# Mixture-of-experts stages: the down product in two-part rounded fp32, weighted by GpSimd

## The chip, the cores and the metric

One core of one Trainium2 chip runs the whole program. The metric is the time of one execution on the device in microseconds; lower is better. The engines are named as the profile names them: PE (TensorE), ACT (ScalarE), DVE (VectorE), POOL (GpSimd) and SP (SyncE, which only issues transfers).

## The reference

A chain of four parts works on 2048 tokens of 128 numbers: a gated layer with running sums (`_L0_attn_a`), two transformer layers (`_L0_ffn`), a non-causal attention (`_L0_attn_b`), and the same two transformer layers again. A transformer layer is causal attention and then a mixture of 8 experts, of which two count:

```python
def _ffn(h, w1, b1, w2, b2):
    return gelu(h @ w1 + b1, approximate=False) @ w2 + b2      # 128 -> 512 -> 128

def _combine_weights(logits):                                  # top 2 of 8, softmax over the two
    vals, idx = top_k(logits, 2)
    w = softmax(vals)
    return sum(w[..., None] * onehot(idx, 8), axis=-2)

def _token_moe(h, ...):                                        # layer 0: per token
    cw = _combine_weights(h @ gw + gb)
    for e in range(8):
        out = out + _ffn(h, w1[e], b1[e], w2[e], b2[e]) * cw[..., e:e + 1]

def _seq_moe(h, ...):                                          # layer 1: one choice for the sequence
    cw = _combine_weights(h.mean(axis=1) @ gw + gb)
    ...
```

All is fp32. Layer 0 computes all eight experts for all tokens and weights them; layer 1 computes only the two that were chosen.

## The kernel before

The program is a row of stages, each with its own semaphores and a barrier at its end. `feed_forward` runs, for each of its two layers, `project_qkv`, `attention_heads`, `finish_attention` and `experts`; it is called twice, with the tag f and with the tag g, and a stage for the separate attention (tag b) lies between. So `experts` runs four times: token-routed (f, then g) and sequence-routed (f, then g). Tiles of the two layers of one tag have the same names in the profile.

`experts` works on four chunks of 512 tokens. First DVE normalises all 16 tiles of 128 tokens into `e_hn`; PE transposes them chunk by chunk into `e_ps_turn`; ACT writes h once into `e_h_hi` as rounded fp32 (`F32R`) and once in place, and DVE subtracts the first from the second to get `e_h_lo` (line 1470). The router's logits follow: 48 small matmuls in the token-routed stage, one in the other, then a chain of small DVE operations (`top2`) that picks the two best.

Then comes a hardware loop over the four chunks (`Fori`), whose body is written out for all blocks. A block is one of the four parts of 128 hidden units of one expert; a chunk has 32 blocks in the token-routed stage and 8 in the other. For block k, PE runs `up(k)`: three matmuls (lines 1559 to 1561), weights stationary, 512 tokens moving: `w1_hi` with `h_hi`, `w1_lo` with `h_hi`, `w1_hi` with `h_lo`. ACT makes the gelu out of PSUM into `e_hidden` (line 1656), plain fp32. Three blocks later PE runs `down(k-3)`: four fp32 matmuls (line 1609), one for each 128 tokens, with the hidden tile stationary and w2 moving, so that the result has the tokens on the partitions. The profile shows each fp32 matmul as two records. After the four blocks of an expert DVE multiplies the sum by the token's combine weight and adds it to `z_tok` (line 1516). The bias b2 comes in by a matmul of the transposed combine weights with the 8 rows of b2 (line 1626) and an addition by DVE (line 1533). In the token-routed stage the combine weights are finished chunk by chunk, with ACT's Exp (line 1660) in each pass.

w2 of the token-routed layer is loaded once, in the set-up (line 201 of the source), and kept in SBUF. In the sequence-routed stage SP loads w1, w2 and b1 of each of the two chosen experts, and DVE waits for all six transfers before it splits both w1 in one go (lines 1500 and 1501).

The semaphores of a stage are cleared by GpSimd at the start of the next (`clear_previous`), ahead of its own work there, which in `project_qkv` and `experts` is `rstd` (line 304), on which the normalisation waits.

## Time and profile before

| | us |
|---|---|
| median of 3 runs | 3347.49 (3345.98 to 3355.19) |
| profiled execution, its own time | 3349.13 |
| its span | 3347.4 |

| engine | busy us | share of the span |
|---|---|---|
| PE matmul | 2748.5 | 82% |
| PE weight load | 1299.9 | 39% |
| DVE | 2337.0 | 70% |
| ACT | 2171.7 | 65% |
| POOL | 331.7 | 10% |

The four `experts` stages lie, with their matmuls, at about 616 to 847 and 2569 to 2799 us (token-routed) and 1306 to 1387 and 3259 to 3343 us (sequence-routed); the last one ends the program. The shares over the whole span say little about them, since attention, which fills most of it, has other limits. What counts is the busy time of each engine inside a stretch of one stage, the granted clock there (1.00 is 2.4 GHz, 0.50 is 1.2 GHz), and at the edges of a stage the order in time of single rows. A matmul's own duration holds its latency; the pace of PE is read from one start to the next.

### The profile page before, as it was taken

To read this page: it belongs to the slowest core of one execution; us is meant where nothing else is said; L and a number is where in the kernel's file an instruction comes from. 1 tells how busy PE (TensorE), PEld (TensorE's weight loads), DVE (VectorE), ACT (ScalarE), POOL (GpSimd) and SP (SyncE) were. 2 spreads that over 40 slices of the span, in tenths; PEclk is the share of its full clock that TensorE was granted. 3 is DMA by queue.
4 is the path that set the end of the run, shared out by engine and by line. 5 is a ranking of instruction groups with operands and counts; after the bars stand their busy time and mean duration, and the time that the engine had idled before them with its cause. 6 is when DMAs were issued, how large, how long until landed. Compare 5 with 4: busy or idle time off the path is not lost. (4 is left out here: it accounts for less than half of the span.)

```text
span 3347.4 us, 75365 instructions
## 1 busy us (share of the span) xinstructions
PE 2748.5 (82%) x29824; PEld 1299.9 (39%) x29824; DVE 2337.0 (70%) x3203; ACT 2171.7 (65%) x4160; POOL 331.7 (10%) x868
## 2 busy tenths in 40 slices
PE   4459999699499994859999998389996996799967
PEld 3322332599333332612222222233333995233326
DVE  5659997322499993469999996499993223799953
ACT  1137889354278983339999998168884453588853
POOL 3023110000031100000000000031100000221000
PEclk8669999799699997969999999699997998799988
DMA  2060000000500001140000000600001003200010
GB/s 56 7 142 27 13 11 8 30 0 0 126 21 15 10 10 45 40 88 8 10 8 10 8 8 25 138 18 16 12 10 32 1 0 75 65 18 11 10 34 25
DMA packets 96737, 99.80 MB, mean 30 GB/s; under 512 B 13158, under 2 KB 84644, under 8 KB 96420
## 3 DMA queue, kind: packets, MB, share of 16 engines
q1 hardware_dynamic: 79140, 77.62, 8.8%
q10 hardware_dynamic: 16640, 15.73, 1.9%
q8 instruction: 214, 3.51, 0.5%
q0 software_dynamic: 640, 2.10, 0.2%
q14 instruction: 103, 0.84, 0.1%
HBM read 51.44 MB, written 43.65 MB: 28 GB/s over the span
## 5 line engine op out<-in xcount | busy, mean ns | idle before, releaser
L1189 ACT ACTIVATE h_probsf<-h_ps_scoresf 128x512 f32<-128x512 f32 (+3 forms) x1216 | 603.5, 552 | 155.3 <-PE h_ps_scoresf L1141 142.9
L1189 ACT ACTIVATE h_probsg<-h_ps_scoresg 128x512 f32<-128x512 f32 (+3 forms) x1216 | 603.6, 552 | 150.8 <-PE h_ps_scoresg L1141 138.3
L1189 ACT ACTIVATE h_probsb<-h_ps_scoresb 128x512 f32<-128x512 f32 x1024 | 556.3, 596 | 73.8 <-PE h_ps_scoresb L1141 63.8
L1163 PE MATMUL h_ps_valuesf<-h_probsf,v_all 128*9 128x256 f32 (+2 forms) x4608 | 348.8, 375 | 29.5 <-POOL h_probsf L1252 21.9
L1163 PE MATMUL h_ps_valuesg<-h_probsg,v_all 128*9 128x256 f32 (+2 forms) x4608 | 347.5, 374 | 26.3 <-POOL h_probsg L1252 18.6
L1163 PE MATMUL h_ps_valuesb<-h_probsb,v_all 128*9 128x256 f32 x4096 | 318.4, 383 | 9.4 <-ACT h_drainedb L1196 4.8
L1212 DVE TENSOR_REDUCE h_maxima_0b<-h_ps_scanb 128x2 f32<-128x1024 f32 x256 | 292.5, 1217 | 10.9 <-PE h_ps_scanb L1103 9.6
L1212 DVE TENSOR_REDUCE h_maxima_2b<-h_ps_scanb 128x2 f32<-128x1024 f32 x256 | 292.8, 1217 | 6.7 <-PE h_ps_scanb L1103 6.7
L1103 PE MATMUL h_ps_scanf<-k_stack,q_stack 48*128 48x512 bf16 (+3 forms) x1280 | 218.1, 363 | 69.9 <-DVE h_ps_valuesf L1201 51.5
L1212 DVE TENSOR_REDUCE h_maxima_0f<-h_ps_scanf 128x2 f32<-128x1024 f32 x224 | 259.2, 1219 | 22.6 <-PE h_ps_scanf L1103 22.3
L1103 PE MATMUL h_ps_scang<-k_stack,q_stack 48*128 48x512 bf16 (+3 forms) x1280 | 217.0, 361 | 70.3 <-DVE h_ps_valuesg L1201 50.4
L1212 DVE TENSOR_REDUCE h_maxima_0g<-h_ps_scang 128x2 f32<-128x1024 f32 x224 | 259.0, 1219 | 20.5 <-PE h_ps_scang L1103 20.2
L1141 PE MATMUL h_ps_scoresf<-q_stack,k_stack 49*128 49x256 bf16 (+2 forms) x2048 | 228.0, 286 | 13.2 <-ACT h_probsf L1189 7.2
L1141 PE MATMUL h_ps_scoresg<-q_stack,k_stack 49*128 49x256 bf16 (+2 forms) x2048 | 227.9, 286 | 12.6 <-ACT h_probsg L1189 6.8
L1103 PE MATMUL h_ps_scanb<-k_stack,q_stack 48*128 48x512 bf16 x1024 | 200.7, 390 | 37.9 <-DVE h_ps_valuesb L1201 21.7
L1141 PE MATMUL h_ps_scoresb<-q_stack,k_stack 49*128 49x256 bf16 x2048 | 201.6, 275 | 15.0 <-ACT h_probsb L1189 14.7
L1212 DVE TENSOR_REDUCE h_maxima_2f<-h_ps_scanf 128x2 f32<-128x1024 f32 x160 | 185.6, 1219 | 12.7 <-PE h_ps_scanf L1103 11.6
L1212 DVE TENSOR_REDUCE h_maxima_2g<-h_ps_scang 128x2 f32<-128x1024 f32 x160 | 185.6, 1219 | 12.7 <-PE h_ps_scang L1103 11.6
L1252 POOL TENSOR_SCALAR_AFFINE_SELECT h_probsg<-h_probsg 128x128 f32<-128x128 f32 (+1 forms) x384 | 122.9, 332 | 621.5 <-ACT h_probsg L1189 614.5
L1252 POOL TENSOR_SCALAR_AFFINE_SELECT h_probsf<-h_probsf 128x128 f32<-128x128 f32 (+1 forms) x384 | 122.0, 332 | 598.3 <-ACT h_probsf L1189 591.4
L1141 PEld LDWEIGHTS h_ps_scoresf<-q_stack,k_stack 49*128 49x128 bf16 x2048 | 66.3, 94 | 261.5 <-ACT h_probsf L1189 238.9
L1141 PEld LDWEIGHTS h_ps_scoresg<-q_stack,k_stack 49*128 49x128 bf16 x2048 | 66.3, 94 | 259.5 <-ACT h_probsg L1189 239.7
(423 smaller groups left out, 3865.9 us busy)
## 6 DMA issues: line engine op xcount, KB each, us to landing
q_stack<-q_parts ACTq DMA_DIRECT2D x20, 256.0 KB, 8.3
k_stack<-k_parts ACTq DMA_DIRECT2D x20, 256.0 KB, 9.8
q_stack<-q_parts SPq DMA_DIRECT2D x20, 256.0 KB, 8.8
k_stack<-k_parts SPq DMA_DIRECT2D x20, 256.0 KB, 10.7
attended<-h_drainedf SPq DMA_DIRECT2D x16, 256.0 KB, 2.3
attended<-h_drainedf SPq DMA_DIRECT2D x32, 128.0 KB, 1.9
attended<-h_drainedb SPq DMA_DIRECT2D x32, 128.0 KB, 1.9
attended<-h_drainedg SPq DMA_DIRECT2D x16, 256.0 KB, 2.2
```

The source lines that it names most:

```text
L1103: last = nc.tensor.matmul(ps_scan[:, i % RING_A, b, at:at + width], m.q_stack[rows, c, 2 * quad + hp, t * P:(t + 1) * P], m.k_stack[rows, ...
L1141: last[b] = nc.tensor.matmul(ps_scores[:, (2 * n_pair + b) % RING_S, width * i + off:width * (i + 1)], m.k_stack[rows, kb // TPC, pair, at ...
L1163: last = nc.tensor.matmul(ps_values[32 * j:32 * j + VD, low:high], m.v_all[:, kb, QUAD * quad + j, :], probs[:, (u + j % banks) % RING_P, ...
L1189: nc.scalar.activation(by_head(probs[:, of % RING_P, :], of), by_head(ps_scores[:, of % RING_S, :], of), ACT.Exp, scale=SOFTMAX_SCALE).the ...
L1212: nc.vector.tensor_reduce(found[:, :, low], now, AXIS_X, ALU.max).then_inc(freed, 1)
L1252: nc.gpsimd.affine_select(out=at, in_=at, compare_op=ALU.is_ge, fill=0.0, base=0, pattern=[[0, at.shape[1]], [1, P]], channel_multiplier=- ...
```

## The change

- The down product is computed as the up product is: `w2_hi` and `w2_lo` stationary, the hidden tile split in `hidden_hi` and `hidden_lo` moving, three matmuls of 512 columns. The result has the 128 output dimensions on the partitions.
- The split of the hidden tile: for even blocks ACT makes the gelu in place in PSUM and DVE rounds it (`high`); for odd blocks ACT makes it twice, into `hidden_hi` and in place. DVE subtracts (`low`) for all blocks.
- w2 is loaded in each stage into two buffers and split by GpSimd.
- ACT moves an expert's result out of PSUM with b2 as bias (`evacuate`). In the token-routed stage GpSimd multiplies it by the combine weights and adds it up over the experts. The weights of a chunk are transposed, written to DRAM, and read back spread over all partitions, one row of 512 for each expert. In the sequence-routed stage the weight is the scale of the evacuation, and GpSimd adds the two experts.
- PE transposes the sum of a chunk back (`turn_back`), and DVE adds it to `z`. The b2 matmuls, the additions per expert and the statistics after the last stage are gone.
- All combine weights are finished at once, in blocks 3 to 6 of the first chunk.
- The order: four ups run ahead of the downs (three before); in the token-routed stage they stand ahead of the logits. The hardware loop is gone; all blocks are written out. Normalising is done by chunks in two buffers.
- In the sequence-routed stage the two w1 are asked for first, then the biases, then w2; each w1 is split when it is in.
- Many small tiles are put into the space of `q_stack`; `w_qkv`, `w_swiglu` and `w_out` are kept only as long as they are used. In the profile such tiles go by the name `q_stack`.

```diff
@@ set_up
-            rest.append((m.b2[:, :, :], ins["L0_ffn_e_b2"].rearrange("l e d -> e l d")))
-            sp.dma_start(m.w2[:, :, :, :], ins["L0_ffn_e_w2"][0].rearrange("e (i p) d -> p (e i) d", p=P))
+                     (rows[E_B2:N_VEC, :], ins["L0_ffn_e_b2"][0])]
@@ experts
+RING_H, RING_SPLIT, RING_CW, RING_W2 = 4, 4, 4, 2
+LAG = 4
+CW_AT, TURN_BACK_AT = 8, 8
@@ gpsimd
+            for e in range(n_exp):
+                pool.wait_ge(w2_in[e], 16)
+                now = raw_w2[:, e % RING_W2, :]
+                nc.gpsimd.tensor_copy(w2_hi[:, e, :], now).then_inc(w2_high, 1)
+                pool.wait_ge(w2_high, e + 1)
+                nc.gpsimd.tensor_tensor(w2_lo[:, e, :], now, w2_hi[:, e, :].bitcast(F32), ALU.subtract)
+            for y in range(CHUNKS * n_exp):
+                c, e = y // n_exp, y % n_exp
+                pool.wait_ge(evacuated, y + 1)
...
+                if by_token:
+                    pool.wait_ge(cw_in[y % RING_CW], 16 * (y // RING_CW + 1))
+                    nc.gpsimd.tensor_tensor(part, y_sb[:, y % 2, :], cw_rows[:, y % RING_CW, :], ALU.mult)
+                    if e:
+                        nc.gpsimd.tensor_tensor(acc[:, c % 2, :], acc[:, c % 2, :], part, ALU.add)
+                elif e:
+                    nc.gpsimd.tensor_tensor(acc[:, c % 2, :], y_sb[:, 0, :], y_sb[:, 1, :], ALU.add)
@@ vector
+            def high(k):
+                dve.wait_ge(gelu_ready, k + 1)
+                if k >= RING_SPLIT:
+                    dve.wait_ge(down_ready, k + 1 - RING_SPLIT)
+                nc.vector.tensor_copy(hidden_hi[:, k % RING_SPLIT, :], ps_h[:, k % RING_H, :])
+            def low(k):
+                nc.vector.tensor_tensor(hidden_lo[:, k % RING_SPLIT, :], ps_h[:, k % RING_H, :],
+                                        hidden_hi[:, k % RING_SPLIT, :].bitcast(F32), ALU.subtract)
...
+            for k in range(total):
+                if k % 2 == 0:
+                    high(k)
+                low(k)
+                if by_token and k == 3:
+                    choose()
+                if by_token and k == 6:
+                    combine()
@@ tensor
-                    for r in range(TPC):
-                        q = slice(r * P, (r + 1) * P)
-                        last_ = nc.tensor.matmul(ps_y[:, e % 2, r, :], hidden[:, k % ring_h, q], w2[:, e, b, :],
-                                                 start=b == 0 and r == 0, stop=b == FB - 1, skip_group_check=True)
+                product(ps_y[:, y % 2, :], (w2_hi[:, e, b * D:(b + 1) * D], w2_lo[:, e, b * D:(b + 1) * D]),
+                        (hidden_hi[:, k % RING_SPLIT, :], hidden_lo[:, k % RING_SPLIT, :]), b == 0, b == FB - 1)
...
+            for k in range(RING_H, total):
+                up(k)
+                down(k - LAG)
+                if by_token and k == CW_AT:
+                    turn_cw(0)
+                if by_token and k % blocks == 2 * CW_AT and k // blocks + 1 < CHUNKS:
+                    turn_cw(k // blocks + 1)
+                if k >= blocks and k % blocks == TURN_BACK_AT - 1:
+                    turn_back(k // blocks - 1)
@@ scalar
+            def gelu(k):
+                act.wait_ge(up_ready, k + 1)
+                if k % 2:
+                    if k >= RING_SPLIT:
+                        act.wait_ge(down_ready, k + 1 - RING_SPLIT)
+                    nc.scalar.activation(hidden_hi[:, k % RING_SPLIT, :], ps_h[:, k % RING_H, :], ACT.Gelu, bias=bias)
+                    act.wait_ge(high_by_act, k // 2 + 1)
+                nc.scalar.activation(ps_h[:, k % RING_H, :], ps_h[:, k % RING_H, :], ACT.Gelu, bias=bias)
+            def evacuate(y):
+                act.wait_ge(down_ready, FB * (y + 1))
+                if y >= 2:
+                    act.wait_ge(weighted, y - 1)
+                nc.scalar.activation(y_sb[:, y % 2, :], ps_y[:, y % 2, :], ACT.Identity, ...)
```

PE, in the first token-routed stage, inside the loop: two blocks of before. `e_ps_h` is the PSUM tile of an up product, `e_ps_y` that of a down product, the letter f at a name's end the tag.

```order
1255 L1609 MATMUL e_ps_yf<-w,e_hiddenf 128x128 x4
1256 L1559 MATMUL e_ps_hf<-e_h_hif,w_hi 128x512
1257 L1560 MATMUL e_ps_hf<-e_h_hif,w_lo 128x512
1258 L1561 MATMUL e_ps_hf<-e_h_lof,w_hi 128x512
1259 L1603 REGISTER_ALU
1260 L1609 MATMUL e_ps_yf<-w,e_hiddenf 128x128 x4
```

The same place now, from the last logit on; four ups have run before the logits.

```order
1240 L1608 MATMUL e_ps_turnf<-gate_hi,e_h_hif 128x8
1241 L1609 MATMUL e_ps_turnf<-gate_hi,e_h_lof 128x8
1242 L1610 MATMUL e_ps_turnf<-gate_lo,e_h_hif 128x8
1243 L1608 MATMUL e_ps_hf<-e_h_hif,w_hi 128x512
1244 L1609 MATMUL e_ps_hf<-e_h_hif,w_lo 128x512
1245 L1610 MATMUL e_ps_hf<-e_h_lof,w_hi 128x512
1246 L1608 MATMUL e_ps_yf<-e_hidden_hif,e_w_hif 128x512
1247 L1609 MATMUL e_ps_yf<-e_hidden_hif,e_w_lof 128x512
1248 L1610 MATMUL e_ps_yf<-e_hidden_lof,e_w_hif 128x512
```

The four matmuls of 128 columns have become three of 512, and the first down follows the first up behind the logits at once.

SP, in the sequence-routed stage of f, before: the loads of the first chosen expert, then a register load for the second.

```order
217 L1672 TENSOR_LOAD ids_int
218 L1672 ISA x2
219 L1673 ISA
220 L1673 DMA e_raw_w1f<-in_L_ffn_e_w 128x512
221 L1675 DMA e_w2f<-in_L_ffn_e_w 128x4x128
222 L1677 ISA
223 L1677 DMA e_b1f<-in_L_ffn_e_b 128x4x1
224 L1672 TENSOR_LOAD ids_int
```

And now, behind both register loads:

```order
232 L1795 DMA q_stack<-in_L_ffn_e_w 128x512
233 L1795 ISA
234 L1795 DMA q_stack<-in_L_ffn_e_w 128x512
235 L1798 ISA
236 L1798 DMA e_b1f<-in_L_ffn_e_b 128x4x1
237 L1800 ISA
238 L1800 DMA e_b2f<-in_L_ffn_e_b 128x1
239 L1798 ISA
240 L1798 DMA e_b1f<-in_L_ffn_e_b 128x4x1
241 L1800 ISA
242 L1800 DMA e_b2f<-in_L_ffn_e_b 128x1
243 L1803 DMA q_stack<-in_L_ffn_e_w 128x4x128 x2
```

Both w1 stand first and both w2 last.

POOL, at the start of the projection that follows a token-routed stage, before and now; the ISA rows are the semaphores that `clear_previous` clears.

```order
109 L1404 UNCONDITIONAL_BRANCH
110 L644 UNCONDITIONAL_BRANCH
111 L95 ISA x29
112 L304 TENSOR_TENSOR rstd<-p_tmpb,neg_half 128x16
113 L587 UNCONDITIONAL_BRANCH
```

```order
159 L1394 UNCONDITIONAL_BRANCH
160 L640 UNCONDITIONAL_BRANCH
161 L96 ISA x51
162 L300 TENSOR_TENSOR rstd<-p_tmpf,neg_half 128x16
163 L583 UNCONDITIONAL_BRANCH
```

Ahead of `rstd` there were 29 such instructions behind each of the first three `experts` stages (the rows of before are those behind a sequence-routed one); now there are 51 behind a token-routed stage and 45 behind the sequence-routed one.

## Rows read from the trace of the kernel before

**Rows 1.** Stretches of the token-routed stage: busy time (count) by engine, clock, DMA.
```profile
625.00:635.00 10.00, 10.00 (x48) 10.00 (x49) 0.00 (x0) 0.30 (x1) 0.00 (x0) 0.50 0.01 2
635.00:639.00 4.00, 4.00 (x10) 3.16 (x11) 3.41 (x12) 1.38 (x2) 0.00 (x0) 0.50 0.00 0
639.00:690.00 51.00, 51.00 (x359) 46.68 (x358) 10.01 (x37) 25.04 (x35) 0.00 (x0) 1.00 0.00 1
```

**Rows 2.** Timeline: start us, duration us, engine, line, operation.
```profile
690.15 0.39 PE L1559 MATMUL e_ps_hf<-e_h_hif,w_hi 128*128 x1
...
690.85 0.40 PE L1559 MATMUL e_ps_hf<-e_h_hif,w_hi 128*128 x1
...
839.11 0.48 PE L1559 MATMUL e_ps_hf<-e_h_hif,w_hi 128*128 x1
...
840.69 0.48 PE L1559 MATMUL e_ps_hf<-e_h_hif,w_hi 128*128 x1
```

**Rows 3.** Groups by line, ACT, 600 to 870 us: busy us, mean ns | idle before.
```profile
L1656 ACT ACTIVATE e_hiddenf<-e_ps_hf,vecs 128x512 f32<-128x512 f32 x128 | 87.6, 688 | 113.3 <-PE e_ps_hf L1561 113.0
...
L1660 ACT ACT_TABLE_LOAD x4 | 5.1, 1283 | 0.1
...
L1638 ACT ACTIVATE e_h_hif<-e_ps_turnf,vecs 128x512 fp32r<-128x512 f32 x4 | 3.1, 773 | 30.3 <-PE e_ps_turnf L1553 30.3
```

**Rows 4.** Groups by line and form, DVE, whole span.
```profile
L1470 DVE TENSOR_TENSOR e_h_lof<-e_ps_turnf,e_h_hif 128x512 fp32r<-128x512 f32 x8 | 5.5, 690 | 6.1 <-ACT e_ps_turnf L1641 6.1
...
L443 DVE TENSOR_SCALAR a_ega<-a_ps_paira 128x512 f32<-128x512 f32 x4 | 2.8, 692 | 0.2
...
L452 DVE TENSOR_SCALAR a_ega<-a_ega 128x512 f32<-128x512 f32 x4 | 1.7, 414 | 0.0
```

**Rows 5.** Groups by line and form, POOL, whole span.
```profile
L1034 POOL TENSOR_TENSOR w_lo<-h_raw_weightsf,w_hi 128x512 fp32r<-128x512 f32 x8 | 10.1, 1269 | 0.7
...
L1032 POOL CAST w_hi<-h_raw_weightsf 128x512 fp32r<-128x512 f32 x8 | 4.9, 611 | 7.0 <-DMA h_raw_weightsf<-in_L_ffn_e_w 7.0
```

**Rows 6.** Timeline, end of the token-routed stage and start of the next projection.
```profile
843.04 3.73 PE L1609 MATMUL e_ps_yf<-w,e_hiddenf 128*128 128x128 f32 x32
...
849.35 0.19 DVE L292 TENSOR_TENSOR p_tmpf<-st 128x16 f32<-128x16 f32 x1 [0.30 <-PEq L1404]
...
850.64 0.17 DVE L298 SCALAR_TENSOR_TENSOR p_tmpf<-p_tmpf 128x16 f32<-128x16 f32 x1
851.39 2.91 POOL L304 TENSOR_TENSOR rstd<-p_tmpf,neg_half 128x16 f32<-128x16 f32 x1 [236.54 <-DVE p_tmpf L298]
```

**Rows 7.** Timeline, PE, second pass: combine weights transposed, and the b2 products.
```profile
697.03 0.60 PE L1619 MATMUL e_ps_turnf<-ident,e_cw_nowf 128*8 128x128 f32 x4
...
699.14 1.15 PE L1626 MATMUL e_ps_turnf<-b,e_cw_tf 8*128 8x128 f32 x8
```

**Rows 8.** Timeline, DVE beside POOL: in the set-up, and in the first attention.
```profile
12.81 6.92 POOL L234 MEMSET k_stack<- 32x8192 f32 x1
...
17.28 2.48 DVE L250 CAST gate_hi<-gate_w 128x16 fp32r<-128x16 f32 x1 [6.56 <-DMA b<-in_L_ffn_e_b]
...
253.77 3.48 DVE L1219 TENSOR_REDUCE h_maxima_0f<-h_ps_scanf 128x8 f32<-128x1024 f32 x3
...
254.43 1.27 POOL L1034 TENSOR_TENSOR w_lo<-h_raw_weightsf,w_hi 128x512 fp32r<-128x512 f32 x1
```

**Rows 9.** Timeline, sequence-routed stage of f: first load, first and last matmul, next stage.
```profile
1320.38 0.37 SPq L1673 DMA_DIRECT2D e_raw_w1f<-in_L_ffn_e_w  x1
...
1329.08 0.79 PE L1559 MATMUL e_ps_hf<-e_h_hif,e_w_hif 128*128 x1 [6.14 <-DVE e_w_lof L1501]
...
1385.78 0.94 PE L1609 MATMUL e_ps_yf<-e_w2f,e_hiddenf 128*128 128x128 f32 x7
...
1390.13 0.19 DVE L292 TENSOR_TENSOR p_tmpb<-st 128x16 f32<-128x16 f32 x1 [0.30 <-PEq L1404]
```

**Rows 10.** Transfers: KB each, median us from issue to landing.
```profile
e_raw_w1f<-in_L_ffn_e_w SPq DMA_DIRECT2D x2, 256.0 KB, 2.9
```

More of the change, by code:

```diff
@@ L1400, in experts @@
     blocks = n_exp * FB
-    ring_h = 4
-    turn_at = 6 if by_token else 0
-    lag = 3
+    total = CHUNKS * blocks
     with ExitStack() as ctx:
@@ new lines, in _ @@
+            normalise_chunk(0)
+            normalise_chunk(1)
+            for c in range(CHUNKS):
+                split_h(c)
+                if c + 2 < CHUNKS:
+                    normalise_chunk(c + 2)
+            if not by_token:
+                choose_experts()
+            for k in range(total):
[6 more added lines that the diff above has]
+                    combine()
+                c, b = divmod(k - TURN_BACK_AT - 1, blocks)
+                if c >= 1 and b == 0:
+                    add(c - 1)
@@ L1546, in _ @@
+            for c in range((total - TURN_BACK_AT - 2) // blocks, CHUNKS):
+                add(c)
         @block.tensor
@@ L1634, in _, with keep_h @@
+            for k in range(total - LAG, total):
+                down(k)
+            turn_back(CHUNKS - 1)
         @block.scalar
         def _(act):
-            for c in range(CHUNKS):
+            def keep_h(c):
                 act.wait_ge(turned, c + 1)
@@ L1666, in experts @@
-        if not by_token:
-            @block.sync
-            def _(sp):
-                sp.wait_ge(cw_set, 1)
+                act.wait_ge(bias_in, 16 * 2 * TOPK)
+            for k in range(total):
+                gelu(k)
+                if by_token and k + 2 < CHUNKS:
+                    keep_h(k + 2)
+                if by_token and k == 5:
+                    act.wait_ge(top_ready, 1)
+                    nc.scalar.activation(t["ed"], t["d"], ACT.Exp).then_inc(exp_ready, 1)
+                if by_token and k == CW_AT + 1:
+                    keep_cw(0)
+                if by_token and k % blocks == 2 * CW_AT + 1 and k // blocks + 1 < CHUNKS:
+                    keep_cw(k // blocks + 1)
+                if k >= FB - 1 + LAG and (k - LAG) % FB == FB - 1:
+                    evacuate((k - LAG) // FB)
@@ L1680, in _ @@
+                for k, one in enumerate(ones):
+                    sp.dma_start(raw_w2[:, k, :].rearrange("p (i d) -> p i d", d=D), m.ins["L0_ffn_e_w2"][layer, one]
+                                 .rearrange("e (i p) d -> p (e i) d", p=P)).then_inc(w2_in[k], 16)
                 if out is not None:
@@ L1700, in build @@
         m = Memory(nc, ctx, ins)
-        set_up(nc, m, "s")
-        stage_a(nc, m, "a")
+        with ExitStack() as first:
+            for name, blocks in (("w_qkv", 3), ("w_swiglu", 2), ("w_out", 1)):
+                m.turned[name] = first.enter_context(nc.sbuf_tensor(name + "_t", [P, blocks * D], F32))
+            set_up(nc, m, "s")
+            stage_a(nc, m, "a")
         feed_forward(nc, m, "f", load_experts=True)
```

394 lines of the change are left out of this document (221 added, 173 removed).

## The prediction

> **What bounds the kernel now.** The change touches four stretches, all called `experts`: a token-routed one and a sequence-routed one in each of two passes through the feed-forward layers (tags f and g). I read the busy table of stretches first: in 639 to 690 us, inside the first token-routed stage, PE is busy 51.00 of 51.00 us at the full granted clock (1.00, so the upper level of 2.4 GHz), ACT 25, DVE 10, GpSimd nothing [rows 1]. PE alone sets the pace; the loop shortens by what PE's work shortens, until another engine comes within reach. Next the timeline of one block of the loop: its up product starts at 839.11, that of the next block at 840.69, a down product between them: 1.58 us a block [rows 2]. At the start of a pass, where ups stand alone, one up starts at 690.15 and the next at 690.85: 0.70 us for three matmuls of 512 columns, 0.23 each, with rounded fp32 on both sides [rows 2]. So a down product now costs 1.58 - 0.70 = 0.88.
>
> **The down product.** After the change it is again three matmuls, 128x128 weights stationary, 512 rounded columns moving: the very form of the up product, so 0.70. A block falls from 1.58 to 1.40, an expert (four blocks) from 6.32 to 5.61.
>
> **Do the others keep up?** Each must do its new work for an expert inside PE's 5.61.
> ACT: two plain gelus and two pairs of gelus (odd blocks, once into `hidden_hi`, once in place), six at 0.69 [rows 3], plus one evacuation, nearest row the Identity of the same size at 0.77 [rows 3]; with 0.03 between them, 5.1. It fits with 0.5 to spare. In the order its rows show no table load beside the evacuations.
> DVE: four subtractions and two casts. The nearest to the subtraction is the same operation on h, one operand in PSUM and one in SBUF, 0.69; to the cast, a one-input operation that reads PSUM, 0.69 [rows 4]: 6 x 0.72 = 4.3. Idle before, so nothing is displaced.
> GpSimd: a product and a sum, 1.27 each [rows 5]: 2.5 of 5.61, hidden.
> The ring of four: up(k+4) waits for low(k). The longest way, gelu behind a pair and an evacuation, then cast and subtraction, is about 3.5 us after up(k) ends; up(k+4) starts 4.9 after it. PE stays the bound.
>
> **Token-routed stage, from logits to the last matmul.** Before: the 48 logit matmuls fill 625 to 635 at clock 0.50 [rows 1]; the last matmul ends at 843.04 + 3.73 = 846.77 [rows 6].
> After: four ups go ahead of the logits, cheap because PE waits there for h. But the last `keep_h` now stands behind gelu(0) and the pair of gelu(1) on ACT and a table load of 1.28 [rows 3]: 3.3 us more ACT work, some 0.6 of it in old gaps, so the logits start 2.7 later and end at 637.8. Then 124 ups and 128 downs at 0.70 = 176.4; four combine-weight transposes sets and three turn-backs, each four transposes, nearest the x4 at 697.03, 0.60 with its latency; a matmul of 0.40 makes way for the next after 0.23, so the latency is 0.17 and a set 0.43: 3.0 [rows 2, 7]. The b2 products (about 1.1 each, the x8 at 699.14) are gone [rows 7]. And one new stall: `turn_cw(0)` stands behind down(4) and waits for the combine weights. DVE needs about 4.1 for the top-2 choice (12 of its operations fill 3.41 of the 4 us after 635 [rows 1]), then ACT's Exp with a table load before and after it (2 x 1.28), gelu(6), cast, subtraction, 1.5 for the combine: ready some 10.7 after the logits. PE has 7 us of work until then: 3.8 lost, once a stage. Before, this chain ran beside the first blocks. Last matmul: 637.8 + 176.4 + 3.0 + 3.8 = 821.0, 25.8 sooner.
>
> **Its start.** GpSimd's split of w2 (cast 0.61, subtraction 1.27 [rows 5]) now begins just when DVE normalises. The trace shows that the two can exclude each other: a DVE cast of 128x16, SBUF to SBUF, lasted 2.48 us and ended with GpSimd's memset (12.81 + 6.92 = 19.73) [rows 8]. The normalisation is of that kind (SBUF to SBUF, as the 0.41 us TENSOR_SCALAR, against 0.69 where the input is PSUM [rows 4]). Bounds: nothing, if DVE's four go between two GpSimd operations, to 3.8, if they alternate through the splits of two experts. I take 1.5, since DVE's are short and queued back to back. Everything behind shifts by it.
>
> **Its end.** Before, DVE is through at 849.05 (the next stage's first operation at 849.35 had 0.30 of idle time before it), 2.3 after the last matmul [rows 6]. After: for the last two experts GpSimd has four operations in a row, of which 4.6 us lie behind the last matmul, then four transposes with their latency 0.6, an addition 0.70 and the statistics 0.87: 6.8. Loss 4.5.
> Net for a token-routed stage: 25.8 - 1.5 - 4.5 = 19.8; two of them 39.6.
>
> **Sequence-routed stage.** Before, w1 is asked for at 1320.38, yet the split waits for all six transfers, the first up starts at 1329.08 and the last matmul ends at 1385.78 + 0.94 = 1386.72 [rows 9]. After, the two w1 go first and each is split alone, so up(0) starts when the first is in: both register loads and a transfer (median 2.9 [rows 10]) plus a half split of about 1, some 3 us sooner, at 1326.2. w2 comes last, is split by GpSimd (1.9), and lets down(0) start at about 1331.3; the four ups fit ahead of it. Then 28 ups and 32 downs, 60 x 0.70 = 42.0, three turn-backs 1.3, and 0.9 of small waits: 1375.5. That is 11.2 sooner. The tail grows from 3.1 (to 1389.83, again 0.30 before the next stage's first operation [rows 9]) to 5.1, since evacuation, GpSimd's sum and the transposes come before the additions. Net 9.2, and a little less if the clock rises later than in this stage; for f and g together I take 18.
>
> **The semaphores.** At the start of every stage GpSimd clears those of the stage before, one instruction each. The order shows 29 after an experts stage before, and 51, 45 and 51 now. `rstd` of the next projection started at 851.39, though DVE had begun there at 849.35 and had the input ready at 850.81 [rows 6]: 2.0 us for 29, 0.07 each, and already the last on that path. So 22, 16 and 22 more cost 1.5 + 1.1 + 1.5 = 4.1.
> **Set-up**: one small load more and w2's 2 MB out of the queue's end; GpSimd's memset ends later than the loads [rows 8], so nothing.
> **Sum**: 39.6 + 18 - 4.1 = 53.5. From the profiled execution's own 3349.1: 3295.6; it lies 1.6 above the median of the three runs (3347.5), so **3294**.
>
> **A rule beside the rows.** SBUF accesses of DVE and GpSimd: the Trainium skill, "SBUF — State Buffer", section "Who interferes with whom" and the list above it, says that the two share one pair of ports under an exclusive lock, taken by a DVE operation in a two-port mode or with two SBUF inputs, and that the loser waits for the whole instruction. By that rule the 2.48 us cast agrees, the normalisation collides, and casts and subtractions that read PSUM don't; by the opposite reading the third rival below holds.
>
> **Rivals.**
> (1) ACT becomes the bound. Its pairs wait for their own first half. At 0.80 a gelu the expert takes 5.6, as PE; at 0.85, 5.9: 0.3 x 32 and 0.3 x 8 a stage, 24 in all, 3317. For it: ACT would be busy nine tenths. Against: back-to-back gelus are 0.69. 11%.
> (2) The rounded product is no cheaper with a moving operand that was written just before, or its stationary loads show: 0.88 stays, 2 x (128 + 32) x 0.175 = 56 lost: 3350, no change. Against: the up product moves h that ACT and DVE wrote, at 0.70. 5%.
> (3) Slower: the lock in the loop. If DVE's six operations an expert also wait while GpSimd works, DVE needs 4.3 + 2.5 = 6.9 an expert, above PE's 5.61 and above the 6.32 of before: 1.3 x 31 = 40 a token-routed stage, 3374. It decides from 1.3 us of waiting an expert, half of GpSimd's time. For it: the 2.48 us cast. Against: three DVE reductions from PSUM took 3.48 us from 253.77, with GpSimd's 1.27 us subtraction beside them [rows 8]. 7%.
>
> **How the numbers follow.** The forecast has 77%. Its own terms: the start lock 0 to 3.8 twice (+3 to -5), logits at the full clock (4 us twice, +8), after the 3.8 us of idle PE possibly a few us at 0.50, as at 635 to 639 [rows 1] (2 to 4 twice, -8), ACT slightly late (-6): 3280 to 3315. Taking in most of rival 1: **3279 to 3322**. Faster by over 0.3% (10 us, about what can be told from no change here) 0.87, within 0.06, slower 0.07.
>
> **What would show it.** Up and down products start 0.70 apart in the profile of after; PE busy over 98% in the loops, ACT 0.87 to 0.9, DVE 0.76, GpSimd 0.45; one PE gap of about 4 us before the first combine transposes; first normalisations of a token-routed stage longer than 0.35 us; `rstd` of the next stage about 3.5 us after its block begins. Wrong it would be if gelus in the loop wait for nothing while PE waits for `low`, or if DVE's operations there last well over 0.7 us beside GpSimd's.

## The result

| | before | after |
|---|---|---|
| median, us | 3346.73 (3344.93 to 3355.19, 4 runs) | 3304.85 (3296.16 to 3311.28, 4 runs) |
| profiled execution, its own time | 3349.13 | 3296.16 |
| its span | 3347.4 | 3294.4 |

The ratio is 0.9868, with a 95% interval of 0.9838 to 0.9898: 42 us faster. The forecast was 3294 with a range of 3279 to 3322. The sum was made for a profiled execution and gave 3295.6; the profiled one took 3296.2, but it was the shortest of its four, and the median is 8.7 us longer. That these two agree within 0.6 us is luck, as the stretches will show. So two things need an account: how 53 us came about against 53.5 in the sum, and what spreads the runs.

### The profile page after: what moved, and what is told of

Read it like the earlier page. It is cut to its first block and busy times, and to the rows that moved or that the text cites. A ratio compares the mean times of both kernels' runs of the same rounds, so it can differ in the third digit from the quotient of the medians.

```text
span 3294.4 us, 71887 instructions
## 1 busy us (share of the span) xinstructions
PE 2673.7 (81%) x28144; PEld 1180.8 (36%) x28144; DVE 2570.5 (78%) x3323; ACT 2276.4 (69%) x4368; POOL 533.6 (16%) x1036
## 5 line engine op out<-in xcount | busy, mean ns | idle before, releaser
L1159 PE MATMUL h_ps_valuesg<-h_probsg,v_all 128*9 128x256 f32 (+2 forms) x4608 | 348.8, 375 | 26.0 <-POOL h_probsg L1248 18.5
L1208 DVE TENSOR_REDUCE h_maxima_0g<-h_ps_scang 128x2 f32<-128x1024 f32 x224 | 259.0, 1218 | 20.4 <-PE h_ps_scang L1099 20.2
```

What stands on the lines that cost most here:

```text
L1159: last = nc.tensor.matmul(ps_values[32 * j:32 * j + VD, low:high], m.v_all[:, kb, QUAD * quad + j, :], probs[:, (u + j % banks) % RING_P, ...
L1208: nc.vector.tensor_reduce(found[:, :, low], now, AXIS_X, ALU.max).then_inc(freed, 1)
```

## The profile after

The first of DVE's small operations for the mean and variance marks where a stage begins. Below is the view of that line: count, durations in ns (least, median, most), first and last start. Before (line 292):

```profile
...
L292 DVE TENSOR_TENSOR p_tmpf<-st x2: 186/186/187, 146.9 to 849.4; 128x16 f32<-128x16 f32 x2
L292 DVE TENSOR_TENSOR e_tmpf<-st x2: 188/188/188, 610.4 to 1300.8; 128x16 f32<-128x16 f32 x2
L292 DVE TENSOR_TENSOR p_tmpg<-st x2: 186/186/186, 2105.5 to 2802.2; 128x16 f32<-128x16 f32 x2
L292 DVE TENSOR_TENSOR e_tmpg<-st x2: 187/187/187, 2563.2 to 3253.4; 128x16 f32<-128x16 f32 x2
...
L292 DVE TENSOR_TENSOR p_tmpb<-st x1: 186/186/186, 1390.1 to 1390.1; 128x16 f32<-128x16 f32 x1
```

And after (line 288):

```profile
...
L288 DVE TENSOR_TENSOR p_tmpf<-st x2: 186/186/186, 145.8 to 831.0; 128x16 f32<-128x16 f32 x2
L288 DVE TENSOR_TENSOR e_tmpf<-st x2: 184/186/188, 609.5 to 1287.5; 128x16 f32<-128x16 f32 x2
L288 DVE TENSOR_TENSOR p_tmpg<-st x2: 186/186/187, 2082.7 to 2759.3; 128x16 f32<-128x16 f32 x2
L288 DVE TENSOR_TENSOR e_tmpg<-st x2: 185/186/188, 2538.8 to 3214.4; 128x16 f32<-128x16 f32 x2
...
L288 DVE TENSOR_TENSOR p_tmpb<-st x1: 185/185/185, 1367.4 to 1367.4; 128x16 f32<-128x16 f32 x1
```

The differences of neighbouring starts are the lengths of the stretches:

| stretch | before | after | change | the prediction's |
|---|---|---|---|---|
| up to the first projection | 146.9 | 145.8 | -1.1 | 0 |
| projection and attention, layer 0, f | 463.5 | 463.7 | +0.2 | 0 |
| token-routed experts, f | 239.0 | 221.5 | -17.5 | -19.8 |
| projection and attention, layer 1, f | 451.4 | 456.5 | +5.1 | +1.5 |
| sequence-routed experts, f | 89.3 | 79.9 | -9.4 | -9.2 |
| separate attention, its projection and the one behind | 715.4 | 715.3 | -0.1 | +1.1 |
| attention, layer 0, g | 457.7 | 456.1 | -1.6 | 0 |
| token-routed experts, g | 239.0 | 220.5 | -18.5 | -19.8 |
| projection and attention, layer 1, g | 451.2 | 455.1 | +3.9 | +1.5 |
| sequence-routed experts, g | 94.0 | 80.0 | -14.0 | -8.8 |
| sum | | | -53.0 | -53.5 |

The sum agrees because misses of up to 5.2 us, on both sides, cancel. The table says where to look: the token-routed stages gave 2.3 and 1.3 less, the stretch behind each took 3.6 and 2.4 more, and one sequence-routed stage gave 5 more. One stretch of one profile is a rough measure: the projection and attention of layer 0, f, whose code is the same in again and fourth below, took 463.0 and 468.0 us there.

**The loop.** Stretches of the first token-routed stage, columns as in [rows 1]:

```profile
631.00:639.00 8.00, 8.00 (x51) 7.75 (x51) 4.34 (x9) 1.35 (x2) 1.32 (x2) 0.71 0.01 2
639.00:651.00 12.00, 8.33 (x34) 6.33 (x33) 8.16 (x23) 7.88 (x11) 0.00 (x0) 0.89 0.00 0
...
750.00:810.00 60.00, 60.00 (x265) 48.66 (x264) 45.35 (x71) 47.34 (x76) 27.11 (x21) 1.00 0.15 45
```

In the last row, deep in the loop, PE is busy 60.00 of 60.00 us, DVE 0.76, ACT 0.79, GpSimd 0.45 of the time. The timeline of one block (columns as in [rows 2]), with DVE's cast and GpSimd's product and sum among it:

```profile
816.27 0.40 PE L1608 MATMUL e_ps_hf<-e_h_hif,w_hi 128*128 128x512 f32 x1
...
816.97 0.39 PE L1608 MATMUL e_ps_yf<-e_hidden_hif,e_w_hif 128*128 128x512 f32 x1
...
817.21 1.30 POOL L1478 TENSOR_TENSOR q_stack<-q_stack 128x512 f32<-128x512 f32 x1 [2.86 <-ACT q_stack L1735]
...
817.66 0.40 PE L1608 MATMUL e_ps_hf<-e_h_hif,w_hi 128*128 128x512 f32 x1
...
817.71 0.69 DVE L1511 CAST e_hidden_hif<-e_ps_hf 128x512 fp32r<-128x512 f32 x1 [0.46 <-ACT e_ps_hf L1726]
...
818.59 1.30 POOL L1483 TENSOR_TENSOR q_stack<-q_stack 128x512 f32<-128x512 f32 x1
```

Up to down is 0.70, down to up 0.69: a block takes 1.39 against 1.58 [rows 2]. DVE's operations that read PSUM keep their 0.69 beside GpSimd: the cast at 817.71 lies wholly inside GpSimd's product.

**The start.** DVE and GpSimd in the first microseconds, then the last logits at either clock, then the stall. The eight normalisations of the first two chunks, and the four of chunks 2 and 3:

```profile
614.03 4.88 DVE L1498 TENSOR_SCALAR q_stack<-z_tok,mean,rstd 128x128 f32<-128x128 f32 x8 [3.04 <-POOL rstd L300]
614.64 1.26 POOL L1468 TENSOR_TENSOR e_w_lof<-q_stack,e_w_hif 128x512 fp32r<-128x512 f32 x1
...
621.29 2.20 DVE L1498 TENSOR_SCALAR q_stack<-z_tok,mean,rstd 128x128 f32<-128x128 f32 x4
...
624.02 3.58 DVE L1498 TENSOR_SCALAR q_stack<-z_tok,mean,rstd 128x128 f32<-128x128 f32 x4
...
631.15 0.34 PE L1608 MATMUL e_ps_turnf<-gate_hi,e_h_hif 128*128 128x8 f32 x1
...
634.59 0.25 PE L1608 MATMUL e_ps_turnf<-gate_hi,e_h_hif 128*128 128x8 f32 x1
...
634.90 0.36 PE L1610 MATMUL e_ps_turnf<-gate_lo,e_h_hif 128*128 128x8 f32 x1
...
638.31 0.77 PE L1608 MATMUL e_ps_hf<-e_h_hif,w_hi 128*128 128x512 f32 x1
...
650.65 0.60 PE L1663 MATMUL e_ps_turnf<-ident,q_stack 128*8 128x128 f32 x4 [3.67 <-DVE q_stack L1371]
...
652.19 0.63 PE L1609 MATMUL e_ps_yf<-e_hidden_hif,e_w_lof 128*128 128x512 f32 x1
```

GpSimd's subtraction has its usual 1.26; it is DVE that is stretched. In this stage the logits begin 21.6 us after the stage's start (before 14.4), but run at 2.4 GHz for 3.5 us and end 28.8 after it (before 24.7); in that of g they begin at 20.3. The stall is there, 3.67 us, and right behind it matmuls last 0.63 instead of 0.39: the clock is back at 1.2 GHz until 655.2.

**The end.** The last products, GpSimd's queue, and the next stage:

```profile
823.43 0.40 PE L1610 MATMUL e_ps_yf<-e_hidden_lof,e_w_hif 128*128 128x512 f32 x1
...
826.68 1.26 POOL L1483 TENSOR_TENSOR q_stack<-q_stack 128x512 f32<-128x512 f32 x1
828.00 1.12 PE L1674 MATMUL e_ps_turnf<-ident,q_stack 128*128 128x128 f32 x4 [4.17 <-POOL q_stack L1483]
...
832.33 0.17 DVE L294 SCALAR_TENSOR_TENSOR p_tmpf<-p_tmpf 128x16 f32<-128x16 f32 x1
834.64 2.92 POOL L300 TENSOR_TENSOR rstd<-p_tmpf,neg_half 128x16 f32<-128x16 f32 x1 [6.70 <-issue]
```

From 823.83 to 831.04 less the 0.30 in front it is 6.9 us. `rstd` starts 3.60 us after the block begins (before 2.04 [rows 6]), 2.1 us after its input is ready. The four transposes at 828.00 take 1.12 us, as at the lower clock.

## The experiments

All are variants of the changed kernel, and all lengths of stages below are read as above. Of two numbers for a stage the first is that of tag f; both come from one profile. The runs were made in four groups, each beside the kernel before, whose median there was 3347 us in the first two groups (again to cw_later, and best1, fourth, two, ups_after), 3350 in that of w1_wait, warm_start and warm_tail, and 3354 in that of dve_tail. Across groups the ratios compare better than the times.

**again**: no edit.

> The changed kernel as it is, beside its variants on the same chip. Its four times so far lie at 3296 to 3311 us, wider apart than those of the kernel before. Theory: the spread lies in when TensorE's clock rises and falls. Then time and mean granted clock go together: 0.004 less of the mean clock is 0.008 more of the span at 1.2 GHz, 26 us, which cost half of that, 13 us. Rival: the spread lies in transfers or in waits, and times differ by 10 us at the same mean clock.

Measured: 3300.33 (3295.18 to 3301.40, 4 runs), ratio 0.9853 (0.9830 to 0.9876). Its token-routed stages take 222.5 and 221.5 us, the stretches behind 455.3 and 454.4, the sequence-routed stages 80.2 and 80.1. Time and clock go together: the first four runs of the changed kernel are 3296 at 0.900, 3301 at 0.898, 3308 at 0.896, 3311 at 0.897. Over 30 runs of the kernel before, 3340 to 3358 us at 0.909 to 0.903, a straight line gives 11 us for 0.004 (correlation -0.85), against the 13 expected. So most of the spread goes with the clock, about as much as its lower level costs; that nothing else moves both was not tested, a part is left over, and why the clock differs from run to run stays open.

**split_late**

```
 @@ experts, gpsimd
+            if by_token:
+                pool.wait_ge(hn_ready, CHUNKS)
             for e in range(n_exp):
                 pool.wait_ge(w2_in[e], 16)
```

> In the token-routed stages GpSimd waits with the split of w2 until DVE has normalised all four chunks; the rest is the changed kernel. Theory: the two engines exclude each other there. Then the first eight normalisations take about 2.1 us together instead of 4.88, the two later chunks 1.1 instead of 2.20 and 3.58, the logits start 4 to 5 us sooner, and the whole gains 6 to 10 us over the changed kernel. Rival 1, no exclusion (the slow rows have another cause, such as the loads into the same tile): they stay as long, and the time is the same within 2 us. Rival 2, the exclusion only moves: the split now runs beside DVE's choice of the two experts, 12 operations from SBUF to SBUF, which then last longer than 0.29 us each, and the stall before the combine weights grows by what the start gained.

Measured: 3294.19, ratio 0.9832 (0.9809 to 0.9856). Its timeline, the normalisations and the first logit, then DVE's choice beside GpSimd:

```profile
618.07 2.15 DVE L1500 TENSOR_SCALAR q_stack<-z_tok,mean,rstd 128x128 f32<-128x128 f32 x8 [3.04 <-POOL rstd L300]
...
624.22 1.11 DVE L1500 TENSOR_SCALAR q_stack<-z_tok,mean,rstd 128x128 f32<-128x128 f32 x4
...
630.45 0.27 PE L1610 MATMUL e_ps_turnf<-gate_hi,e_h_hif 128*128 128x8 f32 x1 [1.41 <-DVE e_h_lof L1506]
...
640.54 1.27 POOL L1470 TENSOR_TENSOR e_w_lof<-q_stack,e_w_hif 128x512 fp32r<-128x512 f32 x1
...
640.83 1.13 DVE L1352 TENSOR_TENSOR q_stack<-q_stack 128x128 f32<-128x128 f32 x1
...
642.63 1.28 POOL L1470 TENSOR_TENSOR e_w_lof<-q_stack,e_w_hif 128x512 fp32r<-128x512 f32 x1
642.74 0.29 DVE L1354 TENSOR_REDUCE q_stack<-q_stack 128x16 f32<-128x128 f32 x1
```

The exclusion is shown: 2.15 instead of 4.88, and the logits start 16.9 us after the stage's start instead of 21.6 (in g 16.9 instead of 20.3). Rival 2 is right as well: three operations of the choice take 1.13, 0.70 and 1.00 instead of 0.29, 2.0 us in all. The choice's reduction is not stretched: it keeps its 0.29 inside GpSimd's subtraction. The stages take 220.9 and 216.7: 1.6 and 4.8 less than in again, since in the first the logits ran at 1.2 GHz nearly throughout (granted clock 0.54).

**clears_late**

```
 @@ project_qkv, gpsimd
-            m.clear_previous(pool)
             inverse_root(nc, pool, m, m.rstd[:, :], tmp[:, 0, :], var_ready, rstd_ready, 1)
             ...
+            m.clear_previous(pool)
```

> In the projection stages GpSimd clears the semaphores of the stage before after rstd instead of before it; the rest is the changed kernel. Theory: the clears stand on the path only behind the experts stages. rstd then starts 0.25 us after the last of DVE's small operations instead of 2.1, 2.0 and 2.3 us after it, and the whole gains 5 to 6 us over the changed kernel, 1.5 more than the 4.1 that the added semaphores alone were to cost, since those of before go off the path too. Rival: the projection is bound by its transfers or the clock later on, and nothing is gained (within 2 us).

Measured: 3293.22, ratio 0.9829 (0.9806 to 0.9853).

```profile
840.58 0.17 DVE L294 SCALAR_TENSOR_TENSOR p_tmpf<-p_tmpf 128x16 f32<-128x16 f32 x1
840.84 2.92 POOL L300 TENSOR_TENSOR rstd<-p_tmpf,neg_half 128x16 f32<-128x16 f32 x1 [4.65 <-DVE p_tmpf L294]
```

Where `rstd` waited 2.1 us behind its input it now follows at once. Whether the rest of the projection follows, this run alone doesn't show: its stretches behind the token-routed stages take 455.2 and 452.3 us against 455.3 and 454.4 in again. All profiles together do: with the clears ahead of `rstd` and nothing else changed there, 16 such stretches take 453.2 to 458.9, 455.6 in the mean; with the clears behind it (clears_late, best1, warm_start) six take 451.9 to 455.6, 453.5 in the mean. That is the 2.1 us of the wait, so the rival's bound is not there. (In this profile the token-routed stages took 226.8 and 224.9 with unchanged code: there the logits ran at 1.2 GHz throughout.)

**cw_later**

```
+CW0_AT = 11
-                if by_token and k == CW_AT:
+                if by_token and k == CW0_AT:
                     turn_cw(0)
```

(and `keep_cw(0)` behind block `CW0_AT + 1`)

> The first combine-weight transposes stand three blocks later on TensorE (behind block 11 instead of 8), and so does the copy on ACT; the rest is the changed kernel. Theory 1, the stall of 3.7 us is these transposes alone: it goes, with the 3.4 us at 1.2 GHz right behind it, and each token-routed stage gains 4 to 5 us, 8 to 10 in all. Theory 2, the chain behind the logits has other takers: up(10) waits for low(6), late by ACT's two table loads, and ACT's evacuation of the third expert waits until GpSimd has weighted the first, for which the weights must have gone to DRAM and back. Then each stage gains 0 to 2 us, and the waits show up in these two places.

Measured: 3293.91, ratio 0.9831 (0.9806 to 0.9856); the stages take 218.8 and 218.2, 3.5 less than in again. Waits of 630 to 700 us: us in total, times, longest.

```profile
ACT q_stack L1736 <- POOL q_stack L1479: 2.4, 1, 2.4
...
PE e_ps_hf L1609 <- DVE e_hidden_lof L1519: 1.2, 2, 0.9
```

Both waits of theory 2 show up, but PE loses only 1.2 us to the first and nothing to the second, and the clock no longer falls. The truth lies between the theories. The intervals of these three edits overlap with that of again; what is shown is shown by their rows.

**best1**: the three edits, and `y_sb` with four buffers instead of two in the token-routed stages (`act.wait_ge(weighted, y + 1 - ring_y)`).

> The changed kernel with the three edits of the runs before together (w2 split behind the normalisation, semaphores cleared behind rstd, first combine weights three blocks later) and four buffers instead of two between ACT's evacuation and GpSimd's weighting in the token-routed stages. Theory: the three gains add up, about 6 us each, and the wait of ACT for the first weighting (2.4 us) goes too: 3280 to 3284 against 3300. Rival: the edits take away the same waiting time, and together they gain no more than 8 us.

Measured: 3281.07 (3272.79 to 3283.74), ratio 0.9796 (0.9767 to 0.9825), clear of again's interval. Stages of 214.8 and 214.4. The gains add up: 19 us, and the three alone gave 6, 7 and 6; ACT's wait of 2.4 us for GpSimd is gone from its list.

**fourth** and **two**

```
 @@ experts, tensor, down (fourth)
+                nc.tensor.matmul(ps_y[:, y % 2, :], w2_lo[:, e, b * D:(b + 1) * D], hidden_lo[:, k % RING_SPLIT, :], ...)
 @@ (two)
-                nc.tensor.matmul(out, left[1], right[0], start=False, stop=False, ...)   # w2_lo by hidden_hi
```

> Each down product has a fourth matmul of 512 columns, low part of w2 by low part of the hidden tile; the rest is the changed kernel. Theory: TensorE alone sets the pace of the loops. Then 320 matmuls at 0.23 us are 74 us, and the time goes from 3300 to about 3374. Rival, ACT or VectorE is the bound already or nearly: the matmul goes into TensorE's waits, and the time rises by less than 40 us.

> Each down product leaves out its matmul of the low part of w2 by the high part of the hidden tile, so a part of the computation is missing; the rest is the changed kernel. TensorE's work for an expert falls from 5.54 to 4.62 us. Theory: TensorE alone sets the pace, ACT is busy 4.4 us of an expert (0.79 of the time in the loop) and VectorE 4.2. Then nearly all of 74 us is gained, 3226 to 3235. Rival, ACT's or VectorE's way (gelu, cast, subtraction, next up) becomes the bound between the two: only 20 to 50 us are gained, and TensorE waits for the low part.

Measured: 3377.88 and 3247.25, one run each. The fourth matmul costs 78 us, all of its 74 and chance: PE is the bound. Leaving one out gives 53, not 74. In its loop:

```profile
690.00:740.00 50.00, 48.96 (x215) 38.57 (x213) 42.03 (x70) 44.67 (x73) 23.44 (x19) 1.00 0.20 57
```

PE is still busy 0.98 of the time, with ACT at 0.89. The token-routed stages give 24.0 and 20.2 of 29.5 us, the sequence-routed ones 4.4 and 4.9 of 7.4. The traces show where the rest went. Inside each token-routed loop PE waits some 2.8 us more than in again (in the row above 1.04 of 50.00), mostly for DVE's `e_hidden_lo`, as the rival had it. The wait before the combine weights, set by DVE and ACT, is 4.3 and 3.9 us instead of 3.7. And the clock is at 1.2 GHz for longer: in g the logits ran at it throughout and took 10.3 us instead of 7.2. So a matmul less begins to meet the next bound, while one more costs its full price.

**ups_after**

```
-                turn(0), turn(1); for k in range(RING_H): up(k), turn(k + 2); logits()
+                turn(0..3); logits(); for k in range(RING_H): up(k)
```

(with ACT's `keep_h(2)` and `keep_h(3)` ahead of the first gelu)

> In the token-routed stages the first four ups stand behind the logits again, and ACT writes all of h before the first gelu, as in the kernel before; the rest is the changed kernel. Theory: ups ahead of the logits let the logits start later (gelus and a table load stand before the last part of h) but take four ups, 0.7 to 1.3 us each, out of the time behind them. Undoing it lets the logits start 3 to 5 us sooner and adds 3 to 5 us behind them: 0 to 6 us slower than the changed kernel in all. Rival: the order costs more than it brings, as ACT's work stands on the path, and undoing it gains 5 us or more.

Measured: 3308.34, ratio 0.9872 (0.9845 to 0.9899), 8 us slower than again, stages of 225.6 and 225.9. The logits start at 20.3 and 20.7 us, within the 20.2 to 21.6 of after and again: the chunks were late from the normalisation, not from the gelus. And the logits run at 1.2 GHz throughout, as in the kernel before, where nothing but transposes runs ahead of them either. The interval of the whole time overlaps with again's.

**w1_wait**

```
                 for k in range(TOPK):
                     dve.wait_ge(w1_in[k], 16)
+                    dve.wait_ge(w2_in[k], 16)
+                dve.wait_ge(bias_in, 16 * 2 * TOPK)
+                for k in range(TOPK):
```

> In the sequence-routed stages VectorE splits both w1 only when all eight loads are in, with w2 and the biases, as before it waited for its six; the rest is the changed kernel. Theory: the first split now waits for the last transfer, asked for 3.3 us later than the first, so the first up product starts 3.5 to 4 us later, and the time grows by 6 to 8 us over the changed kernel's 3300 (two stages). Rival: the sequence-routed stage is bound behind it by w2, which GpSimd splits only when it is in: the first ups only wait less, and under 3 us are lost.

Measured: 3310.37, ratio 0.9885 (0.9866 to 0.9905), 10 us slower, with an interval that overlaps with again's; the sequence-routed stages take 85.6 and 86.5 instead of 80.2 and 80.1.

```profile
1315.17 1.27 DVE L1557 CAST e_w_hif<-q_stack 128x512 fp32r<-128x512 f32 x1 [6.85 <-DMA q_stack<-in_L_ffn_e_w]
...
1317.37 1.50 DVE L1557 CAST e_w_hif<-q_stack 128x512 fp32r<-128x512 f32 x1
...
1317.60 0.77 PE L1611 MATMUL e_ps_hf<-e_h_hif,e_w_hif 128*128 128x512 f32 x1 [9.47 <-DVE e_w_lof L1558]
```

The order of loads is worth 5.4 and 6.4 us a stage, more than the 4 expected. In f the first up starts 30.8 us after the stage's start instead of 25.1: 4.5 of this is the wait for the last transfer, and 1.1 comes since the late split of w1 by DVE meets GpSimd's of w2, where a cast takes 1.27 and 1.50 us instead of 0.43.

**warm_start** and **warm_tail** (on best1)

```
 @@ experts, tensor (warm_start; 10, 3, one behind every second logit tile, 8)
+                    nc.tensor.matmul(ps_y[:, 1, :], m.w1_hi[:, 0, 0:P], m.w1_hi[:, 0, :], start=True, stop=True, ...)
 @@ experts, tensor, ahead of the last turn_back (warm_tail; 14), and project_qkv, ahead of transpose_chunk(0) (16)
+                    nc.tensor.matmul(ps_h[:, 3, :], m.w1_hi[:, 0, 0:P], m.w1_hi[:, 0, :], start=True, stop=True, ...)
```

> The kernel of best1 with matmuls that compute nothing needed (512 columns, rounded fp32) where TensorE waits at the start of an experts stage: ten and three ahead of the first products of the token-routed stage, one after every second tile of the logits, eight ahead of the first product of the sequence-routed stage. Theory: TensorE's clock rises behind products of 512 columns in a row and falls during the logits, which move 8 columns each. With the added matmuls the logits and the first products run at 2.4 GHz, and a token-routed stage gains 2 to 4 us, a sequence-routed one 1 to 2: 3271 to 3277 against 3281. Rival: the clock falls by a rhythm of its own, whatever TensorE does; then the added matmuls delay the logits by 1.6 to 3.4 us a stage, and the time is 3283 to 3288.

> The kernel of best1 with matmuls that compute nothing needed where TensorE waits for GpSimd's last weightings (14 of 512 columns behind the last down product of a token-routed stage) and for rstd at the start of the four later projections (16). Theory: behind a token-routed stage the changed kernel's projection is longer than before's by more than the semaphores cost (455 to 456.5 us from its start to the next experts stage against 451.3), because TensorE is idle for 15 us instead of 9 and the clock rises later. With the added matmuls this stretch comes down to 450 to 452, and the whole gains 4 to 8 us on the 3281 of best1. Rival: the stretch is longer for another reason (transfers, or chance in the clock of attention), and stays within 2 us.

Measured: warm_start 3285.82, ratio 0.9809 (0.9788 to 0.9831), stages of 219.1 and 219.1; warm_tail 3272.65 (3272.54 to 3281.97), ratio 0.9773 (0.9755 to 0.9792), with stretches of 452.2 and 450.7 where best1 has 455.6 and 453.2. In warm_start the clock does come up early, and is lost in the logits all the same:

```profile
621.40:626.40 5.00, 3.45 (x18) 2.33 (x16) 2.03 (x6) 4.89 (x8) 3.43 (x4) 0.97 0.05 16
626.40:631.40 5.00, 3.54 (x18) 3.35 (x18) 4.22 (x7) 2.53 (x4) 3.88 (x5) 0.72 0.40 119
631.40:636.40 5.00, 5.00 (x22) 4.71 (x22) 0.24 (x1) 0.00 (x0) 3.92 (x5) 0.50 0.38 113
```

The theory of warm_start falls: one product of 512 columns after every second tile does not hold the clock while the logits run. What would is open. The time is where the rival put it (3283 to 3288), but that the clock has a rhythm of its own isn't shown by that: the added matmuls delay the logits under either theory. The sequence-routed stages gained 0.4 and 0.6 us (79.8 and 79.4), less than the 1 to 2 expected. That of warm_tail holds. The projection's first four products of 512 columns took 3.62 us from 841.72 after the change, 3.23 before it, and here they take:

```profile
839.13 1.88 PE L733 MATMUL p_ps_qkf<-p_h_tf,w_dh 128*128 128x512 f32 x4
```

The first 25 us of that projection before, after, and in warm_tail (columns as in [rows 1]; the number behind the last count is the granted clock, 0.64 in best1):

```profile
849.40:874.40 25.00, 13.93 (x50) 8.67 (x51) 11.95 (x39) 7.82 (x12) 2.91 (x1) 0.73 0.19 65
```

```profile
831.00:856.00 25.00, 12.27 (x39) 7.68 (x40) 10.16 (x36) 6.01 (x9) 2.92 (x1) 0.62 0.19 64
```

```profile
831.40:856.40 25.00, 19.61 (x70) 12.28 (x71) 12.96 (x42) 9.09 (x14) 2.92 (x1) 0.81 0.30 93
```

The clock is shown by these rows; the gain in time less firmly. warm_start has best1's projection without the filling, and its stretches were 452.6 and 451.9. Over all profiles the mean is 453.5 without the filling (six stretches) and 450.3 with it (four, 448.0 to 452.2). The median is 8 us lower than best1's, yet the intervals of the ratios overlap, and the profiled execution of warm_tail was the longest of its four. The filling stands in two places, behind the stage and ahead of the projection; which of them does it was not separated.

**dve_tail** (on warm_tail)

```
 @@ experts, vector, ahead of the last add (GpSimd's loop ends one expert sooner)
+                step(nc.vector.tensor_tensor(y_sb[:, y % ring_y, :], y_sb[:, y % ring_y, :], cw_rows[:, y % RING_CW, :], ALU.mult))
+                dve.wait_ge(weighted, y)
+                nc.vector.tensor_tensor(acc[:, 1, :], acc[:, 1, :], y_sb[:, y % ring_y, :], ALU.add)
```

> The kernel of warm_tail in which VectorE, not GpSimd, multiplies and adds the very last expert of a token-routed stage (512 columns, both operands in SBUF), and 8 added matmuls instead of 14 fill TensorE's shorter wait. Theory: the end of such a stage is GpSimd's queue, four operations of 1.26 to 1.30 us for the last two experts. With the last two on VectorE at 0.69 each, of which the product can lie beside GpSimd's, the last transposes start 1.4 to 1.9 us sooner, twice: 3269 to 3270 against the 3272.7 of warm_tail. Rival: the two engines exclude each other, so VectorE's product waits until GpSimd's sum is done, or holds it up; then the gain is 1.2 us a stage or less, and the time is within 1 us of warm_tail's.

Measured: 3271.34 (3269.72 to 3278.15, 5 runs), ratio 0.9760 (0.9747 to 0.9773): the fastest version, 2.4% under the kernel before and some 30 us under the changed one.

```profile
2732.36 1.30 POOL L1491 TENSOR_TENSOR q_stack<-q_stack 128x512 f32<-128x512 f32 x1
2732.81 1.39 DVE L1605 TENSOR_TENSOR q_stack<-q_stack 128x512 f32<-128x512 f32 x1 [1.78 <-ACT q_stack L1756]
2734.23 0.69 DVE L1608 TENSOR_TENSOR q_stack<-q_stack 128x512 f32<-128x512 f32 x1
```

The rival's mechanism was right: DVE's product takes 1.39, its end 0.54 behind GpSimd's. The last transposes start 2.9 us after the last product instead of 4.3 in warm_tail, 1.3 sooner, between the rival's 1.2 and the theory's 1.4. The whole time is within what two runs of the same kernel differ by.

## Why the prediction was right, and where it was not

**Bound and product: right.** Both products take 0.69 to 0.70, PE has no gap in the loop, and fourth shows that a matmul more costs all of itself. The kind of product was read off the up product [rows 2] and that held for a moving operand written just before. DVE at 0.76 and GpSimd at 0.45 came as forecast.

**ACT: too high.** Its 5.1 us an expert are 0.79 x 5.54 = 4.4. The evacuation was priced at 0.77, from the Identity with a scale [rows 3], and is 0.68; a gelu in place is 0.66, and two of them back to back take 1.24. So rival 1 had 1.2 us of room, not 0.5. In two, ACT is at 0.89, about what the forecast expected of the kernel itself.

**The start: the sum right by luck.** 2.7 for ACT's work and 1.5 for the lock made 4.2, and the logits end 4.1 later. In truth they start 7.2 later. Without the lock (split_late) it is 2.5, so the 2.7 was right; the lock was mis-sized: 4.7 in this stage, 3.4 in that of g. I took 1.5 of bounds that ended at 3.8, since I counted the first eight normalisations (2.7 lost) and left out those of chunks 2 and 3 (1.1 and 2.5), on which the last `keep_h` hangs. The 2.7 and the lock don't simply add up either: with the lock in place, taking ACT's work away (ups_after) brings the logits no sooner. And 3.1 came back because the clock was up when the logits began, which stood in the range but not in the sum. It is not sure to come: in the profile of clears_late the ups run ahead as well, the clock stays down through the logits, and the stages are 3 to 5 us longer, as in ups_after.

**The stall: right** (3.67 against 3.8), though both of its sides were short: the combine weights came 12.3 us behind the logits, not 10.7, and PE had 8.7 us of work until then, not 7, since its first matmuls ran at 1.2 GHz. What it drags along was only in the range: 3.4 us at 1.2 GHz, in which eight matmuls lose 0.2 us each. The first eight behind the logits, too, were counted at the full clock. From the end of the logits to the last matmul it took 185.5 us instead of 183.2: 1.6 and 1.5 for these two, 0.4 for a wait ahead of the last product (its start 0.60 behind the matmul before instead of 0.23), less 1.3 for the pace (0.695 a product over the whole loop) and 0.1 for the stall; 0.2 is left.

**The end: right** (6.9 against 6.8), **rstd: nearly** (3.60, 3.46 and 3.89 us after the block's start, 2.04 before: 4.8 in all instead of 4.1). clears_late shows that the whole wait of `rstd` behind its input can go.

**What the sum left out** is a term that the prediction had only for the stall and put at nothing here: what PE's longer wait at the end does to the clock of the stage behind it. PE is idle or nearly so from 823.8 to the projection's transposes at 838.8, 15 us against 8.7 before. The projection then runs longer at 1.2 GHz: +5.1 and +3.9 us where the semaphores alone explain 1.6 and 1.9, with a granted clock of 0.62 over its first 25 us against 0.73 before. warm_tail fills the wait, the clock is 0.81 there, and the stretches come down from best1's 455.6 and 453.2 to 452.2 and 450.7, in dve_tail, with less filling behind the stage, to 448.0 and 450.4. That the clock changes is shown; how many of the 3.5 and 2.0 us it explains is not, as single stretches vary by as much.

**Sequence-routed stage: right for f** (the first up 25.1 us after the stage's start, forecast 25.4; the last matmul at 74.3, forecast 74.7), where w1_wait confirms the order of loads. For g the miss is in the kernel before, whose products ran at 1.2 GHz from 3282 to 3291 us, against some 3.5 us after the change (granted clock 0.65 over 3239 to 3244, 1.00 behind). The first part of it (columns as in [rows 1]):

```profile
3282.00:3287.00 5.00, 4.91 (x15) 3.65 (x15) 0.00 (x0) 1.38 (x2) 0.00 (x0) 0.50 0.00 0
```

I had read f alone and doubled it, less a little.

**The rivals.** None came. The third, the lock in the loop, is out by the 0.69 us of DVE's operations beside GpSimd's 1.30. In these traces the lock bites where both of DVE's inputs are in SBUF, and in casts and normalisations from SBUF to SBUF; the choice's reduction, from SBUF to SBUF too, kept its 0.29. The rule that stood beside the prediction, from the Trainium skill, "SBUF — State Buffer", section "Who interferes with whom", draws this line too (a DVE operation in a two-port mode or with two inputs in SBUF, against GpSimd), and the traces agree with it in four places: the normalisation, the choice in split_late, the cast in w1_wait and the product in dve_tail.

## What to carry to other kernels

Work given to an engine that was idle isn't free: ask at each edge of a stage what else runs there, above all DVE's casts, normalisations and two-input operations on SBUF beside GpSimd, and what instructions stand ahead of the one that the path waits for. A wait of TensorE cost its own length here and then some of the products behind it at half the clock, in the next stage too. A sum that comes out right says little about its terms; compare stretch by stretch.

## What was not expected of the hardware

- The two engines exclude each other for up to several times the length of the shorter operation: eight normalisations 4.88 instead of 2.15 us, casts of 128x512 from SBUF to SBUF 1.27 and 1.50 instead of 0.43, an operation of the choice 1.13 instead of 0.29; but a reduction kept its 0.29. GpSimd mostly keeps its 0.6 and 1.26 to 1.30; in w1_wait one of its casts took 0.81 and one subtraction 1.60.
- The granted clock falls, or stays down, during the logits, 48 matmuls of 8 columns, with PE busy 5.00 of 5.00 us; in the profile of after it fell 3.5 us into them, in warm_start with products of 512 columns among them.
- A semaphore cleared by GpSimd costs 0.07 to 0.09 us: `rstd` starts 2.04 us after its block behind 29 of them, 3.46 behind 45, 3.60 and 3.89 behind 51.
